# Audio tower kernel: scheduling of the eight attention steps, of the router's broadcasts, and of the experts' two layers on TensorE

## What is computed

```python
scores = x @ tok_w + tok_b                      # keep the 204 best rows of 256, in order of score
h = x[top] * sigmoid(top_scores)
h = h + attention(layernorm(h))                 # one head of 64, softmax over 204 rows, output projection
h = h + ffn(layernorm(h))                       # 8 experts, top 2 of a router, softmax of the two logits
# expert e:  y_e = gelu(xn @ W1[e] + b1[e]) @ W2[e] + b2[e],  W1[e] 64x128, W2[e] 128x64
# every expert is computed for every row; y = sum over e of y_e * weight_e (zero where not chosen)
```

## Time and profile before

| | |
|---|---|
| median of 3 runs | 236.09 us (234.95 to 238.71) |
| profiled execution, its time | 235.3 us |
| its span (first to last instruction) | 233.2 us |
| PE busy | 212.2 us (91% of the span), 1672 matmul records |
| DVE, ACT, POOL busy | 160.9, 144.1, 148.8 us |
| granted PE clock | 0.993 on the mean |
| first expert matmul / last output job on PE | 108.75 / 228.61 us from the span's start |

### The profile page before, as it was taken

One profiled execution on the slowest core, in us unless ns is written; L12 is line 12 of the kernel. 1 busy time (PEld: TensorE's weight loads), 2 busy tenths in 40 slices (PEclk: granted clock), 3 DMA queues, 4 the chain that ended last, 5 costly groups with the idle time before them and its releaser, 6 DMA issues. The chain is left out here.

```text
span 233.2 us, 5334 instructions
## 1 busy us (share of the span) xinstructions
PE 212.2 (91%) x1672; PEld 115.5 (50%) x1672; DVE 160.9 (69%) x540; ACT 144.1 (62%) x368; POOL 148.8 (64%) x193
## 2 busy tenths in 40 slices
PE   1788989999999999998999999899999999799981
PEld 0545777676766676765344434244344433244320
DVE  7999999997989896738344745738474554464362
ACT  2736758787878685959836654555558365555730
POOL 3869848869786868505048974667656546556571
PEclk9999999999999999999999999999999999999997
DMA  4257540606050501116738329256293493856701
GB/s 110 47 183 183 89 134 1 174 3 191 22 165 3 148 17 41 38 54 160 158 76 214 77 62 218 48 147 148 60 233 82 115 218 98 203 118 147 171 15 39
DMA packets 18570, 25.71 MB, mean 110 GB/s; under 512 B 5102, under 2 KB 15598, under 8 KB 18542
## 3 DMA queue, kind: packets, MB, share of 16 engines
q10 hardware_dynamic: 6324, 13.61, 24.8%
q1 hardware_dynamic: 12218, 11.76, 19.6%
HBM read 23.40 MB, written 1.96 MB: 109 GB/s over the span
## 5 line engine op out<-in xcount | busy, mean ns | idle before, releaser
L1363 DVE SCALAR_TENSOR_TENSOR ye<-PD,b_col,mb 128x408 f32<-128x408 f32 (+1 forms) x65 | 40.9, 633 | 47.5 <-PE PD L1053 40.3
L722 ACT ACTIVATE hid<-PD,b_eff 128x816 f32<-128x816 f32 x64 | 56.8, 940 | 26.1 <-PE PD L1038 18.9
L519 POOL TENSOR_TENSOR acc<-acc,ye 128x408 f32<-128x408 f32 x52 | 54.6, 1050 | 25.1 <-DVE ye L1363 22.0
L1038 PE MATMUL PD<-uT,w_g 64*128 64x408 f32 x256 | 53.1, 531 | 2.3 <-ACT hid L722 1.3
L1053 PE MATMUL PD<-hid,w_sb 128*64 128x408 f32 x256 | 51.4, 519 | 1.3 <-DVE ye L1363 1.2
L1038 PEld LDWEIGHTS PD<-uT,w_g 64*128 64x128 f32 x256 | 21.8, 186 | 21.6 <-ACT hid L722 9.2
L1053 PEld LDWEIGHTS PD<-hid,w_sb 128*64 128x64 f32 x256 | 15.5, 136 | 33.4 <-issue 28.6
L660 ACT ACTIVATE E<-PD,nmax 102x204 f32<-102x204 f32 x64 | 26.9, 442 | 6.2 <-DVE nmax L1254 6.2
L1217 DVE SCALAR_TENSOR_TENSOR ahead<-srow,score,PD 128x256 bf16<-128x256 f32 x56 | 23.4, 475 | 0.0
L1254 DVE TENSOR_REDUCE nmax<-PD 102x2 f32<-102x408 f32 x32 | 17.1, 576 | 3.1 <-PE PD L947 2.4
L519 POOL TENSOR_TENSOR acc<-H,ye 128x408 f32<-128x408 f32 x8 | 8.4, 1049 | 16.6 <-DVE ye L1363 15.4
(11 more groups left out here) (177 smaller groups left out, 331.0 us busy)
## 6 DMA issues: line engine op xcount, KB each, us to landing
mb<-mixd ACTq DMA_DIRECT2D x28, 408.0 KB, 5.9
srow<-scored SPq DMA_DIRECT2D x7, 512.0 KB, 4.7
rdbc<-rdend SPq DMA_DIRECT2D x16, 102.0 KB, 2.9
rbc<-rstd2d SPq DMA_DIRECT2D x16, 102.0 KB, 2.7
mb<-mixd SPq DMA_DIRECT2D x4, 408.0 KB, 6.2
X<-in_x ACTq DMA_DIRECT2D x6, 256.0 KB, 3.2
out<-y SPq DMA_DIRECT2D x7, 204.0 KB
w_raw<-in_L_ffn_W SPq DMA_DIRECT2D x2, 256.0 KB, 5.9
```

The source lines that it names most:

```text
L519: pool.tensor_tensor(acc[n % 4][:, :], H[:, n, :] if e == 0 else acc[n % 4][:, :], ye[k % 4][:, :], ALU.add)\
L722: act.activation(hid[k % 4][:, :, :], hid_ps[k % 2][:, :, 0:C], ACT.Gelu, bias=b1_eff[:, e:e + 1]).then_inc(hid_ok, 1)
L1038: last = pe.matmul(hid_ps[k % 2][:, p, 0:C], w1_g[halves[p], e, :], uT[halves[p], n, :], start=True, stop=True)
L1363: dve.scalar_tensor_tensor(out=ye[k % 4][:, part], in0=y_ps[k % 2][:, part], scalar=b2_col[:, e:e + 1], in1=mb[n % MB][:, e, part], op0=AL ...
```

## The change

Five things are changed, and all but one are orders.

1. PE in the steps: `variance2_wide` moves behind `scores(s,0)`, `variance2_rows` behind `scores(s,1)`. 2. ACT in the steps: `copy_var2` moves behind `softmax(s,0)`; for steps 1 to 6 `copy_OT(s-1)` moves ahead by one Exp activation, behind the first of the four of `softmax(s,1)`. 3. All `read_mix` go from ACT's queue to SP's, each right behind its `write_mix` (unit 2's halves around `read_std2(6)`); `store(1)` moves behind `write_mix(5)` and its read. 4. The expert loop on PE becomes `hidden(k)`, `second(k-2)`, `hidden(k+1)`, `second(k-1)`. `normalise2(6)` on DVE moves from behind `weighted(15)` to behind `weighted(17)`. 5. The second part of the last `weighted` writes to PSUM (`ye63`) instead of SBUF, and the last add reads it there.

```diff
+        ye63 = PD[1][:, 0, 0:S]
@@ SP
+            def read_whole(n):
+                read_mix(sp, n, 0)
+                read_mix(sp, n, 1)
             write_mix(0)
-            read_mix(sp, 0, 0)
-            read_mix(sp, 0, 1)
+            read_whole(0)
             write_std2(UNITS - 3)
             write_den(UNITS - 1)
             read_std2(UNITS - 3)
             read_den(UNITS - 1)
             write_mix(1)
+            read_whole(1)
             write_mix(2)
             write_std2(UNITS - 2)
+            read_mix(sp, 2, 0)
             read_std2(UNITS - 2)
+            read_mix(sp, 2, 1)
             write_mix(3)
+            read_whole(3)
             write_std2(UNITS - 1)
             read_std2(UNITS - 1)
             write_mix(4)
+            read_whole(4)
             store(0)
+            write_mix(5)
+            read_whole(5)
             store(1)
-            write_mix(5)
             store(2)
             store(3)
             store(4)
             write_mix(6)
+            read_whole(6)
             store(5)
             write_mix(7)
+            read_whole(7)
             store(6)
@@ ACT, steps
-                if (u := unit(s, 2)) is not None:
-                    copy_var2(u)
                 softmax(s, 0)
-                if s < UNITS - 1:
+                if (u := unit(s, 2)) is not None:
+                    copy_var2(u)
+                if s == 0:
                     softmax(s, 1, [0])
-                    if s == 0:
-                        copy_hT(s)
-                    else:
-                        copy_OT(s - 1)
+                    copy_hT(s)
+                    softmax(s, 1, [1])
+                elif s < UNITS - 1:
+                    softmax(s, 1, [0], [0])
+                    copy_OT(s - 1)
+                    softmax(s, 1, [0], [1])
                     softmax(s, 1, [1])
@@ ACT, experts
-                if k in (5, 7):
-                    read_mix(act, 1, (k - 5) // 2)
-                if k >= 15 and k % NE == 7 and k // NE + 1 < UNITS:
-                    read_mix(act, k // NE + 1, 0)
-                if k >= 17 and k % NE == 1 and k // NE < UNITS:
-                    read_mix(act, k // NE, 1)
@@ PE, steps
                 values(s)
-                if (u := unit(s, 2)) is not None:
-                    variance2_wide(u)
                 if s == 1:
                     expert_bias(0, 2)
                 scores(s, 0)
                 if (u := unit(s, 2)) is not None:
-                    variance2_rows(u)
+                    variance2_wide(u)
                 if s == 1:
                     expert_bias(2, 4)
                 scores(s, 1)
+                if (u := unit(s, 2)) is not None:
+                    variance2_rows(u)
@@ PE, experts
             for k in range(2, K, 2):
                 hidden(k)
+                second(k - 2)
                 hidden(k + 1)
-                second(k - 2)
                 second(k - 1)
@@ DVE
-                    dve.scalar_tensor_tensor(out=ye[k % 4][:, part], in0=y_ps[k % 2][:, part], scalar=b2_col[:, e:e + 1],
+                    dve.scalar_tensor_tensor(out=ye63 if done is ye63_ok else ye[k % 4][:, part], in0=y_ps[k % 2][:, part], scalar=b2_col[:, e:e + 1],
                                              in1=mb[n % MB][:, e, part], op0=ALU.add, op1=ALU.mult).then_inc(done, 1)
-                if k == 15:
+                if k == 17:
                     normalise2(UNITS - 2)
-                    dve.tensor_tensor(acc[3][:, 0:S], acc[3][:, 0:S], ye[i][:, 0:S], ALU.add).then_inc(last_ok[0], 1)
+                    dve.tensor_tensor(acc[3][:, 0:S], acc[3][:, 0:S], ye63 if k == K - 1 else ye[i][:, 0:S], ALU.add)\
+                        .then_inc(last_ok[0], 1)
```

More of the change, by code:

```diff
@@ L650, in copy_k, with softmax @@
                 act.activation(kT[:, :, :], qk_ps[:, :, S:2 * S], ACT.Identity, bias=bk_col[:, 0:1]).then_inc(k_ok, 1)
-            def softmax(u, pr, ps=range(2)):
+            def softmax(u, pr, ps=range(2), qts=range(R)):
                 if u >= 1:
@@ L658, in softmax @@
                     act.wait_ge(max_ok, 4 * u + 2 * pr + p + 1)
-                    for qt in range(R):
+                    for qt in qts:
                         last = act.activation(E[pr][:, p, qt, :], S_ps[pr][:, p, qt * S:(qt + 1) * S], ACT.Exp,
@@ L779, in _ @@
                     copy_mT(0)
+                softmax(s, 0)
                 if (u := unit(s, 2)) is not None:
                     copy_var2(u)
-                softmax(s, 0)
-                if s < UNITS - 1:
+                if s == 0:
                     softmax(s, 1, [0])
-                    if s == 0:
-                        copy_hT(s)
-                    else:
-                        copy_OT(s - 1)
+                    copy_hT(s)
[4 more added lines that the diff above has]
+                    softmax(s, 1, [0], [1])
                     softmax(s, 1, [1])
```

## The result

| | before | changed |
|---|---|---|
| median | 235.85 us (4 runs, 234.95 to 238.71) | 240.53 us (4 runs, 240.39 to 241.93) |
| ratio | | 1.0223, 95% interval 1.0179 to 1.0267 |
| profiled execution, time / span | 235.3 / 233.2 us | 240.4 / 238.3 us |
| first expert matmul on PE (`hidden(0)`) | 108.75 us | 106.94 us |
| from there to the last output transposes (start) | 119.86 us | 126.77 us |

The changed kernel is about 2.2% slower. (The ratio and its interval leave out the run of 238.71 us, which belongs to a slower state that executions of this kernel fall into at times.) The forecast was 239.8 us in a range from 236.8 to 242.8. The two profiled spans differ by 5.1 us: the attention steps take 1.8 us less, the expert phase takes 6.9 us more.

What follows compares the result with a forecast made beforehand. PE was taken to bound expert phase and attention steps. From the profiled 235.3 us: -2.9 steps, +10.5 switches, -1.4 and -1.3 waits gone, +0.3 new wait, -0.6 end gave 239.9, stated as 239.8 us; range 236.8 to 242.8.

Steps and rivals of the forecast that it cites:

- changes of shape in 31 iterations: Expert loop on PE: switching between hidden and second twice as often costs 0.35 us an iteration, taken as +10.5 us.
- attention steps: Attention steps: the select_z wait for OT goes, less PE work a step, earlier Exps in step 7; -2.9 us in all.
- wait in iteration k = 20: Expert loop, seconds 18 and 19: the wait behind DVE's stand for rbc goes, -1.4 us.
- wait at hidden(50): Expert loop: the wait for a gelu behind ACT's issue of two mb reads goes, -1.3 us.
- new wait for unit 6's weights: Expert loop: DVE waits some 2 us at weighted(48), nearly covered before second(50); +0.3 us.
- the end: Seconds 62 and 63 and the last add: 0.3 us saved on each, -0.6 us together.
- next bound: Attention steps: DVE, with 0.42 + 0.41 us idle a step, just holds a step 0.5 us shorter.
- The waits that go: Expert loop: PE's waits at k = 20 (1.4 us) and hidden(50) (1.3 us) vanish through moved reads and later normalise2(6).
- The rival of late `mb` reads: Steps gain nothing, or mb reads for units 5 to 7 come late behind stores on SP: 242.3 us, chance 0.28.

Runs made afterwards that it cites:

- e1: The changed kernel with PE's expert loop back in paired order (two hiddens, then two seconds): 230.9 us median, ratio 0.979 to the kernel before.
- e5: The changed kernel, alternating order, with the first layer's matmuls in the second layer's shape (computes something else, for time alone): 227.6 us, one run.
- e6: The changed kernel with both layers in one shape and the expert loop in paired order (computes something else, for time alone): 227.8 us, one run.
- e7: The kernel before with only PE's part of the new step order (variance2_wide and variance2_rows moved): 237.5 us, one run.
- e8: The kernel before with only ACT's part of the new step order (copy_var2 and copy_OT moved): 236.7 us, one run.
- e10: The changed kernel with the expert loop paired again and copy_var2 moved from ACT to DVE, behind row_max(s,1): 231.1 us median, ratio 0.982.
- e2: The kernel before with the alternating expert order on PE alone, reads, normalise2(6) and steps as before: 242.8 us, ratio 1.030.
- e9: The kernel before with the mb reads moved from ACT to SP alone: 233.6 us median of 10, ratio 0.993.
- e4: The kernel before with the new order of the attention steps alone, on PE and ACT: 234.3 us median, ratio 0.997.
- e3: The changed kernel with the alternating order in every second iteration of the expert loop, paired in the others: 236.2 us, ratio 1.001.

## Why the prediction was right, and where not

By its own steps, in us against the profiled execution; "measured" is from the two traces unless an experiment is named:

| term | predicted | measured |
|---|---|---|
| changes of shape in 31 iterations | +10.5 | +10.9 (0.352 each; changed less e1: 10.6, as e1 waits 0.3 at second 62) |
| attention steps | -2.9 | -1.8 |
| wait in iteration k = 20 | -1.4 | -1.4 |
| wait at hidden(50) | -1.3 | -1.5 |
| wait at hidden(42) | left in the range | -0.5 |
| new wait for unit 6's weights | +0.3 | 0 |
| the end | -0.6 | -0.6 |
| sum | +4.6 | +5.1 (spans: +5.1) |

The sum came within 0.5 us partly by luck: the steps are 1.1 us and the changes of shape 0.4 us worse than said, and the waits, which came out 1.0 us better, take most of that back. On the size the prediction leaned the other way than the ratio: it gave 0.60 to a change of less than 2% and 0.35 to a slower kernel beyond that. The ratio is 1.0223, its interval (1.0179 to 1.0267) has 2% in it, so the runs leave this open.

*The switches.* Right in mechanism and size. The lone hidden (0.88) and the inner half of a second (0.34) in the trace of before gave 3.44 us for an iteration, which is what it took. That the shape is the cause was argued then and is shown by e5 and e6.

*The steps.* This is the term that was mis-sized, by 1.1 us, over a third of it. The change of shape that was saved is there: from the start of `values` to the start of `attend` e7 takes 3.05 us (66.76 to 69.81), 0.14 less than with the old order, where 0.17 was said. The wait for OT is gone as said. What the sum missed is the second thing that ACT's chain feeds. The prediction followed ACT up to `copy_OT` and stopped; but an Exp moved from ahead of `copy_OT` to behind it stands ahead of the copy of ET, and `turn_exp` of the next step, which needs that copy, now comes 1.91 us after `select_z` instead of 1.74 (73.47 less 71.73 before). 0.17 us in each of steps 3, 4, 5 and 7, 0.29 in step 6 and 0.36 in step 2 go back that way: 1.3 us, a little more than the term was off. e8, which has ACT's part alone, shows the same loss. Here are the rows of ACT (changed kernel): with the three Exps between them there is no gap from OT to zT, so that in this order ET can't come earlier unless OT does.

```profile
69.95 0.51 ACT L690 ACTIVATE OT<-PD 128x408 f32<-128x408 f32 x1
...
71.58 0.86 ACT L682 ACTIVATE ET<-PD 102x816 f32<-102x816 f32 x1
72.32 0.52 ACT L653 ACTIVATE zT<-PD 128x408 f32<-128x408 f32 x1
```

Against the "next bound" that was named, DVE, e10's trace shows DVE idle for 0.40 us ahead of `copy_v`. In step 7 the experts start 0.2 us earlier relative to their step instead of 0.3: they still wait 0.53 us for the last Exp. The first expert matmul thus came at 106.94 us and not at 106.

*The waits that go.* All three went, but the reason given was only one of two. The prediction credited the reads' move to SP and the later `normalise2(6)`. e2 has neither, and its loop has no wait either: with 0.35 us more for each iteration, PE is late enough. In the paired order the same edits are worth 3.4 us in the loop (119.86 to 116.15, with 0.3 more at the end); e9 shows that the reads alone cure hidden 42 and 50 and half of the wait at seconds 18 and 19, and in e1, which has the later `normalise2(6)` too, the other half is gone. That place was not tried by itself. That `rbc` would come 2 to 4 us later behind 816 KB was wrong; by the traces its second read lands 8.8 us after the write before, 8.2 in e9 and 8.5 in the changed kernel.

*The wait that was to come.* It did not reach PE. Unit 6's weights took 8.7 us from write to first use, not 10.6. In the changed kernel (SP, then DVE) the read is issued 2.1 us after the write, not 3.9:

```profile
198.07 0.57 SPq L363 DMA_DIRECT2D mixd<-mT  x1
200.14 2.38 SPq L302 DMA_DIRECT2D mb<-mixd  x4
```

```profile
206.77 0.64 DVE L1371 SCALAR_TENSOR_TENSOR ye<-PD,b_col,mb 128x408 f32<-128x408 f32 x1 [0.26 <-POOL acc L531]
```

In the kernel before an output store of 204 KB had been issued 1.9 us ahead of this write; that the store held it up was not tried by itself. The rival of late `mb` reads falls with this: no wait of DVE in the changed kernel is put down to `mb`. The margin was next to nothing, though: the second of these reads landed at 206.69, 0.08 us before DVE's use.

*The end.* The last add reads from PSUM and takes 0.37 us instead of 0.69, with POOL's add beside it as before. From second 63 to the last transposes it takes 2.82 us in the profiled kernels with that operand in SBUF (before, e2, e4, e7, e8, e9) and 2.51 in those with it in PSUM (changed, e1, e3, e5, e6, e10).

```profile
233.19 0.37 DVE L1464 TENSOR_TENSOR acc<-acc,PD 128x204 f32<-128x204 f32 x1
```

## What to carry to other kernels

Order matmuls on PE in runs of one shape: here each change costs 0.18 us, which no row shows as idle time and only the distances between starts tell, and an order that looks more even doubled the changes and cost 11 us of 240. When PE is the bound, look in the old trace for a lone instance of the group that is to be split up: here it priced the reordering to 0.01 us an iteration. And when a step of a chain is moved ahead on an engine, follow what it was moved past up to its own consumer; here over a third of the expected gain was missing there.

## What the runs showed of the hardware that was not expected

*A pace of half at full granted clock.* In some executions PE's first step takes 0.8 to 1.3 us longer. In e1 `project`'s first eight records take 0.74 us from start to start (15.50 to 16.24), in the kernel before 0.40 (15.23 to 15.63), with the granted clock recorded as 1.00 in both. First e1, then before:

```profile
15.50 0.96 PE L932 MATMUL PD<-zT,wq_bd 64*64 64x204 f32 x8 [0.30 <-ACT zT L653]
16.24 0.90 PE L932 MATMUL PD<-zT,wk_bd 64*64 64x204 f32 x8
```

```profile
15.23 0.58 PE L924 MATMUL PD<-zT,wq_bd 64*64 64x204 f32 x8 [0.36 <-ACT zT L641]
15.63 0.52 PE L924 MATMUL PD<-zT,wk_bd 64*64 64x204 f32 x8
```

It is over after about 5 us. The same eight records take 0.74 us in the profiled executions of e1, e2, e3, e6, e7, e8, e9 and e10, and 0.40 in those of the kernel before, the changed one, e4 and e5. In e2 and e7 it cost the first step 0.2 us at most, in the other six 0.8 to 1.3. The edits of e1, e2, e3 and e9 lie behind this stretch and can't be the cause. It makes the spans of single executions differ by up to 1.3 us whatever is compared, which is why the expert phase and the steps were compared by their own starts here. Its cause stays open.

*A dip of the clock.* In the profiled execution of e4 the granted clock was 0.52 of full for 10.7 us, near the lower of the clock's two levels (1.2 of 2.4 GHz); PE had been busy for 2.5 of the 3.3 us before, at full clock, and the same instructions ran at full clock in the other profiled kernels (windows view):

```profile
28.00:31.30 3.30, 2.51 (x35) 2.39 (x34) 3.21 (x8) 1.09 (x2) 3.13 (x3) 1.00 0.72 202
31.30:42.00 10.70, 10.70 (x60) 8.28 (x60) 7.61 (x33) 5.91 (x19) 4.55 (x12) 0.52 0.10 33
42.00:52.00 10.00, 10.00 (x114) 6.94 (x114) 7.69 (x24) 7.45 (x26) 5.57 (x5) 1.00 0.34 103
```

`select_z` of step 2 came 16.7 us after that of step 1 there, against 13.0 in the kernel before, and that one execution was 3 us longer than its three neighbours. Why the clock fell stays open.
